# Sixteen graphs through a four-part layer on one core: the first and last six pipeline steps written out call by call, weight loads issued in another order

## Chip, cores and metric

One core of one Trainium2 chip. The metric is the device time of one execution in microseconds; the time before is the median of three runs.

## What is computed

The input is x, sixteen graphs of 512 nodes with 128 features, and adj, a 512 by 512 matrix of weights for each graph. Four parts follow each other, each a layer norm and ReLU, an operation on the graph, and a residual sum:

```
h = relu(norm(x));  x = x + attention(h, adj > 0.5)
    # 4 heads: e = leaky_relu(dst_i + src_j, 0.2), softmax over edges,
    # out = attn @ (h @ W) + bias
h = relu(norm(x));  x = x + max over 7 relations r of A_r @ (h @ W_r + c_r) + b
    # A_r: adj, its transpose, shifts, identity
h = relu(norm(x));  x = x + relu(D @ (adj + I) @ D @ (h @ W.T + b2))
h = relu(norm(x));  x = x + softplus(xn @ W_self + (I - S adj S') @ xn @ W_neigh)
    # xn = norm(h) * gamma + beta
```

## The kernel before

**Tiles.** A graph is a tile of 128 partitions by four blocks of 128 nodes. Its adjacency is 1 MB and comes in by one load into `adj_in` (two buffers), its features by another into `x_in` (two buffers). TensorE transposes the adjacency (`adjacency(t)`, L1200) and ScalarE copies it to `adj_tr` (three buffers, L551).

**Stages of a graph.** (1) Norm and hidden features (`norm0`, `rstd_0`, `hidden0`, `h0_transposed`), projection (`project`, L1221), the scores (`scores`, L892), the top score over all nodes (`top_rows`, `top_score`, `top_all`, L1240), the weights and values (`weights`, `values`), which are split into three bf16 parts (`part_hi`, `part_rest` L926, `part_mid` L621, `part_lo` L934). For each of the four heads a mask says which scores of an edge are positive: heads 0 and 2 on VectorE (L951, called masks here), heads 1 and 3 as signs on ScalarE (`sides`, L633) and one comparison on VectorE (L946). TensorE multiplies the parts with the non-edges (`no_edges`, L1290) and with each head's mask (`head(h)`, L1304), 48 matmuls each. `pair`, `attention`, `residual0`, `norm1` close the stage. (2) `hidden1`, the products A times h (`product_ah`, L1341) and A transposed times h (`product_ath`, L1350), the seven relations (`relation(k)`, L1372 to L1376), and the largest on VectorE (L1015). (3) `hidden2`, `h2_transposed` (L1386), `conv_bias`, `conv_linear` (L1403), `conv_in` (L537, the scaling to y2), `conv_product` (L1419), `conv_relu`. (4) `norm3`, `normal3`, `z_transposed`, `laplace_linear`, `laplace_product` (L1452), `softplus`, `result` (L488), `store`.

**Order.** Each engine has one stream, and semaphores join them. The kernel is a software pipeline written by hand: one loop over steps s for each engine, in which each call is made for graph s minus its stage's offset. So the order within a step is the same in all steps, and at the ends, calls for graphs that don't exist fall away:

```python
for s in range(GRAPHS + DEPTH - 1):       # TensorE, L1456, shortened
    product_ath(at(s - 3))
    ...
    head(3)(at(s - 2))
    laplace_product(at(s - 4))
    h2_transposed(at(s - 3))
```

Ahead of the loops stands the set-up. ScalarE issues the loads of the small weights: `w0c`, two broadcasts of the score vectors to 128 partitions, the edge weights, `w2_in`, the node mask, a broadcast of the first bias, and those of the last part. SyncE issues the graphs' loads and the large weights. TensorE transposes w2 and the mask and sums the edge rows (L1167 to L1171) once ScalarE's seventh load, the mask, has landed. VectorE makes the score columns (`head_weights`), then graph 0's statistics, then the edge rows in three bf16 parts (`edge_rows`, to L1109), two bias operations and a weight sum (`biases`, `laplace_weights`), all ahead of its loop.

## Time and profile before

| what | value |
|---|---|
| median of three runs | 727.64 us (727.63 to 728.45) |
| the profiled execution | 728.84 us |
| its span, first to last instruction | 726.7 us |
| TensorE busy in the span | 670.6 us, 92% |
| VectorE / ScalarE / GpSimd busy | 578.6 / 459.8 / 342.8 us |
| mean granted TensorE clock | 0.974 |
| mean rate of the transfers | 38 GB/s |

The profiled execution lasted 2.1 us longer than its span and 1.2 us longer than the median. A line of the order of time gives the start in us from the span's start, the busy time, the engine, the line of the kernel, what is written and read, and in brackets how long the engine was idle before and what ended that. Overlapping matmuls of a run are merged. The granted clock is a share of 2.4 GHz.

### The profile page before, as it was taken

How to read it: one execution, taken by the hardware profiler on the slowest of the kernel's cores; microseconds unless marked ns; L12 is line 12 of the kernel's file. 1: busy time of each engine (PE TensorE's matmuls, PEld its weight loads, DVE VectorE, ACT ScalarE, POOL GpSimd, SP SyncE). 2: the span in 40 equal slices, each digit the busy share in tenths (PEclk: the TensorE clock that was granted, in tenths of full speed). 3: DMA queues.
4: the chain of work that ended last, by engine and by line, in shares of the span. 5: the costliest groups of instructions: out<-in, count | busy, mean ns of one | idle time of the engine just before them, and what ended most of it. 6: DMA issues, size and time to landing. Idle time of an engine off the chain costs nothing. (4 is left out here: it accounts for less than half of the span.)

```text
span 726.7 us, 20537 instructions
## 1 busy us (share of the span) xinstructions
PE 670.6 (92%) x7714; PEld 550.7 (76%) x7730; DVE 578.6 (80%) x1726; ACT 459.8 (63%) x1137; POOL 342.8 (47%) x423
## 2 busy tenths in 40 slices
PE   2588899999999999999999999999999999999844
PEld 1585778889696978789796969788796969787533
DVE  2866988888889988888989988888989888886431
ACT  1455567767667577767667576767666676754332
POOL 1217255545546365555546265555556365353410
PEclk9779999999999999999999999999999999999987
DMA  8001101030202011020202011020302010000000
GB/s 232 1 3 41 35 23 53 0 88 3 88 3 87 3 39 52 1 89 2 88 3 87 3 48 43 0 91 1 89 2 88 3 62 14 16 2 16 1 15 14
DMA packets 28820, 27.83 MB, mean 38 GB/s; under 512 B 1517, under 2 KB 20530, under 8 KB 28722
## 3 DMA queue, kind: packets, MB, share of 16 engines
q1 hardware_dynamic: 27090, 25.97, 11.7%
q8 instruction: 62, 1.02, 0.6%
q10 hardware_dynamic: 1632, 0.55, 0.4%
q14 instruction: 36, 0.29, 0.1%
HBM read 22.31 MB, written 4.19 MB: 36 GB/s over the span
## 5 line engine op out<-in xcount | busy, mean ns | idle before, releaser
L387 POOL TENSOR_TENSOR rstd<-ve,half_neg 128x4 f32<-128x4 f32 x48 | 52.8, 1101 | 203.0 <-DVE ve L1034 116.3
L1304 PEld LDWEIGHTS ps<-part,pos 128*128 128x128 bf16 x3072 | 100.0, 98 | 3.2 <-DVE pos L946 0.7
L1304 PE MATMUL ps<-part,pos 128*128 128x66 bf16 x3072 | 101.8, 194 | 0.5 <-DVE pos L946 0.5
L951 DVE SCALAR_TENSOR_TENSOR pos<-ps,neg_s,none 128x512 bf16<-128x512 f32 x128 | 87.2, 744 | 10.7 <-issue 10.7
L1015 DVE TENSOR_REDUCE best<-ps 128x128 f32<-128x896 f32 x64 | 68.6, 1086 | 20.4 <-PE ps L1376 18.9
L633 ACT ACTIVATE side<-ps,sd 128x512 bf16<-128x512 f32 x128 | 77.2, 691 | 2.8 <-DVE pos L946 2.8
L1452 PE MATMUL ps<-u,adj_tr 128*128 128x128 f32 x512 | 61.1, 278 | 2.5 <-ACT u L731 2.5
L1452 PEld LDWEIGHTS ps<-u,adj_tr 128*128 128x128 f32 x512 | 58.4, 192 | 3.5 <-ACT u L731 3.5
L1290 PE MATMUL ps<-part,nmask 128*128 128x66 bf16 x1536 | 54.7, 197 | 6.0 <-DVE part L934 6.0
L1290 PEld LDWEIGHTS ps<-part,nmask 128*128 128x128 bf16 x1536 | 52.6, 99 | 9.9 <-issue 9.8
L1341 PE MATMUL ps<-adj_tr,h 128*128 128x512 f32 x128 | 59.4, 607 | 0.0
L1350 PE MATMUL ps<-adj_in,h 128*128 128x512 f32 x128 | 57.6, 592 | 0.0
L542 ACT ACTIVATE h<-x,off,rstd 128x128 f32<-128x128 f32 x128 | 53.2, 506 | 5.9 <-POOL off L390 5.9
L1375 PE MATMUL ps<-w_sb,h1t 128*128 128x384 f32 x128 | 51.7, 486 | 0.8
L1419 PE MATMUL ps<-y,adj_tr 128*128 128x128 f32 x384 | 52.2, 280 | 0.0
L418 POOL TENSOR_TENSOR rstd<-ve,half_neg 128x4 f32<-128x4 f32 x16 | 17.6, 1099 | 73.0 <-DVE ve L1057 73.0
L1419 PEld LDWEIGHTS ps<-y,adj_tr 128*128 128x128 f32 x384 | 48.2, 197 | 0.0
L946 DVE TENSOR_TENSOR pos<-side,none 128x2048 bf16<-128x2048 bf16 x32 | 39.2, 1226 | 9.3 <-PE ps L1304 9.0
L488 POOL TENSOR_TENSOR y_out<-sp,x 128x512 f32<-128x512 f32 x16 | 20.3, 1270 | 55.0 <-DVE sp L1078 55.0
L816 DVE BATCH_NORM_STATS2 st<-x 128x6 f32<-128x128 f32 x192 | 41.6, 279 | 0.7
L551 ACT ACTIVATE adj_tr<-ps 128x512 f32<-128x512 f32 x64 | 38.0, 608 | 4.7 <-PE ps L1200 4.7
L1341 PEld LDWEIGHTS ps<-adj_tr,h 128*128 128x128 f32 x128 | 23.2, 191 | 23.3 <-issue 23.0
(163 smaller groups left out, 1631.4 us busy)
## 6 DMA issues: line engine op xcount, KB each, us to landing
adj_in<-in_adj SPq DMA_DIRECT2D x16, 1024.0 KB, 6.2
x_in<-in_x SPq DMA_DIRECT2D x16, 256.0 KB, 6.5
out_y<-y_out SPq DMA_DIRECT2D x16, 256.0 KB, 6.7
w_sb<-in_L_gnn_W SPq DMA_DIRECT2D x7, 64.0 KB, 4.7
b_sb<-in_L_gnn_b SPq DMA_DIRECT2D x1, 256.0 KB, 8.7
c_rows<-c_parts SPq DMA_DIRECT2D x7, 1.5 KB
w0c<-in_L_gnn_W ACTq DMA_DIRECT2D x1, 64.0 KB, 3.0
a_bc<-in_L_gnn_a_src ACTq DMA_DIRECT2D x1, 64.0 KB, 6.4
```

The lines of the kernel that those rows point to most:

```text
L387: G.tensor_tensor(rstd[:], ve[:], half_neg[:, 0:T], ALU.pow).then_inc(power, 1)
L542: last = A.activation(dst[:, t, :], src[:, t, :], func, scale=scale[:, t:t + 1], bias=offset[:, t:t + 1])
L633: last = A.activation(side[:, t, :], bank(B_SPREAD[h]), ACT.Sign, bias=sd[:, t, 0, h:h + 1])
L951: last = V.scalar_tensor_tensor(pos[0][:, t, :], bank(B_SPREAD[h]), neg_s[:, t, h:h + 1], none[:, t, :], ALU.is_gt, ALU.is_gt)
L1015: V.tensor_reduce(best[:, k, :], ps[:, B_REL[k]:B_REL[k] + 2, :].rearrange("p a n -> p (a n)")[:, 0:RELS * F] .rearrange("p (r f) -> p f r ...
L1290: mm(ps[:, B_HEADS[q] + i // 2, o:o + 2 * VAL].rearrange("p (h v) -> p h v", h=2)[:, :, GRP:VAL], nmask[:, t, i * P:(i + 1) * P], parts[n] ...
L1304: last = mm(ps[:, B_HEADS[q] + i // 2, o:o + VAL], pos[h % 2][:, t, i * P:(i + 1) * P], parts[n][:, t, h, :], start=False, stop=(i % 2 == ...
L1341: last = mm(bank(B_AH), h1[:, t, :], adj_tr[g.three][:, t, :], start=(t == 0), stop=(t == T - 1))
L1350: last = mm(bank(B_ATH), h1[:, t, :], adj_in[g.two][:, t, :], start=(t == 0), stop=(t == T - 1))
L1375: mm(b, h1t[:, blk], w1_sb[:, 4:7, :], start=True, stop=False, skip_group_check=True)
L1419: last = mm(own, left, y2[:, t, :], start=(t == 0), stop=(t == T - 1))
L1452: last = mm(bank(B_AU)[:, i * F:(i + 1) * F], adj_tr[g.three][:, t, i * P:(i + 1) * P], u3[:, t, :], start=(t == 0), stop=(t == T - 1))
```

## The change

The loops now cover ten steps in the middle, with their calls in the same order. The first and the last six steps of each engine are written out as a list of calls, in orders of their own. The offsets grow by one (`DEPTH` 7, `at(s - 3)` becomes `at(s - 4)`), which changes no order by itself. Beside this:

- SyncE issues the last part's weights (four loads that ScalarE issued) behind the second adjacency. In its loop the load of an adjacency now stands behind the store; before, it stood ahead of features and store. The third x tile is loaded behind the edge rows.
- The two score vectors, the first bias and b2 are no longer broadcast by four loads of 64 KB. ScalarE loads them as four rows of 512 bytes ahead of its other loads, and one matmul with a row of ones spreads them over the partitions into PSUM (`broadcast_rows`).
- The sums of `b1` and of `w3` move from VectorE's set-up to GpSimd; the cast of the identity and the split of b2 move behind graph 0's scores on VectorE.
- `h1`, `h1t`, `aht`, `atht`, `sum_rows`, `y2` and `u3` get a second buffer; the four tiles of the softplus become slices of one tile, whose first partition holds the edge rows of the set-up.
- TensorE's waits are written anew for the changed orders; some are added that repeat others in the steady loop.

```diff
-DEPTH = 6
+DEPTH = 7
...
-        h1 = sb("h1", [P, T, F])
+        h1 = [sb(f"h1_{i}", [P, T, F]) for i in range(2)]
...
             load_features(at(0))
             load_adjacency(at(0))
-            load_features(at(1))
...
-            for s in range(2, GRAPHS + DEPTH - 1):
-                load_adjacency(at(s))
-                load_features(at(s + 1))
-                store(at(s - 4))
+            load_weights()
+            load_edge_rows()
+            for s in range(GRAPHS + 5):
+                load_features(later(s))
+                store(at(s - 5))
+                load_adjacency(later(s - 1))
...
+            for n, row in enumerate((a_src.rearrange("h f -> (h f)"), a_dst.rearrange("h f -> (h f)"), bias0, b2)):
+                act.dma_start(rows_in[0:1, n * F:(n + 1) * F], row.rearrange("(o f) -> o f", o=1)).then_inc(s_rows_in, 16)
             act.dma_start(w0c[:, 0:F], w0.rearrange("d h f -> d (h f)")).then_inc(s_heads, 16)
-            act.dma_start(a_bc[:, 0, :], a_src.rearrange("h f -> (h f)").partition_broadcast(P)).then_inc(s_heads, 16)
-            act.dma_start(a_bc[:, 1, :], a_dst.rearrange("h f -> (h f)").partition_broadcast(P)).then_inc(s_heads, 16)
...
+            def broadcast_rows():
+                pe.wait_ge(s_rows_in, 16 * 4)
+                pe.wait_ge(s_setup, 1)
+                mm(bank(B_ROWS_IN), ones_row[:], rows_in[:], start=True, stop=True).then_inc(s_rows_ps, 1)
```

**ScalarE, the start of graph 0 and of graph 1.** `h` is hidden features, `h0t` their transposes, `adj_tr` the transposed adjacency (x4: its four blocks), `side` the signs of a head, `part` a split part, `junk` the row sums of the adjacency. Before:

```order
L542 ACTIVATE h<-x_in,off,rstd 128x128 x4
L580 ACTIVATE h0t,h_sum<-ps 128x512
L551 ACTIVATE adj_tr,sums<-ps 128x512 x4
L589 COPY hv<-ps 128x512
L591 COPY mean<-ps 128x128
L598 ACTIVATE val<-s_rel,shift_c 128x16
L599 ACTIVATE val<-s_rel,shift_c 128x16
L633 ACTIVATE side<-ps,sd 128x512 x4
L614 CAST part<-val 128x1056
L621 CAST part<-rest 128x1056
L563 ACTIVATE junk,sums<-adj_in 128x512 x4
L542 ACTIVATE h<-x_in,off,rstd 128x128 x4
```

And now:

```order
L629 ACTIVATE h<-x_in,off,rstd 128x128 x4
L667 ACTIVATE h0t,h_sum<-ps 128x512
L638 ACTIVATE adj_tr,sums<-ps 128x512
L676 COPY hv<-ps 128x512
L678 COPY mean<-ps 128x128
L685 ACTIVATE val<-s_rel,shift_c 128x16
L686 ACTIVATE val<-s_rel,shift_c 128x16
L638 ACTIVATE adj_tr,sums<-ps 128x512 x3
L701 CAST part<-val 128x1056
L708 CAST part<-rest 128x1056
L720 ACTIVATE side<-ps,sd 128x512 x4
L650 ACTIVATE junk,sums<-adj_in 128x512 x4
```

The weights (`val`) come before three of the adjacency copies, and the signs of head 1 (the first `side`) stand behind both parts instead of ahead of them.

**VectorE, the last set-up before the loop, and graph 0's scores.** `w_both` is the weight sum of the last part, which followed the b2 split; `st`, `mv` and `ve` the statistics of graph 1, `sd` the scores, `none` and `nmask` the non-edges, `smax_t` the top score. Before:

```order
L1121 TENSOR_TENSOR w_both<-w_self,w_both 128x128
L816 BN_STATS st<-x_in 128x6 x4
L820 BN_AGGR mv<-st 128x2 x4
L830 TENSOR_SCALAR ve<-mv 128x4
L892 COPY sd<-ps 128x32
L895 TENSOR_REDUCE smax_p<-sd 128x4
L897 TENSOR_SCALAR neg_s<-sd 128x16
L838 TENSOR_SCALAR none<-adj_tr 128x2048
L904 TENSOR_REDUCE smax_t<-ps 4x1
```

And now, from the end of the edge rows (`c_parts`) to the weights:

```order
L1372 TENSOR_TENSOR c_parts<-late,c_parts 1x896
L1149 COPY sd<-ps 128x32
L1152 TENSOR_REDUCE smax_p<-sd 128x4
L1154 TENSOR_SCALAR neg_s<-sd 128x16
L1073 BN_STATS st<-x_in 128x6 x4
L1077 BN_AGGR mv<-st 128x2 x4
L1087 TENSOR_SCALAR ve<-mv 128x4
L1161 TENSOR_REDUCE smax_t<-ps 4x1
L1172 TENSOR_TENSOR s_rel<-sd,ps 128x16
```

The scores directly follow the edge rows; the statistics of graph 1 stand between them and the top score, and the non-edges come behind the weights.

**TensorE, the drain.** `h` with `ident` are the transposes of graph 14, `b_rows` and `w_t` its bias and linear part, `u` with `adj_tr` graph 13's last product, `y` the convolution of graph 14. Before:

```order
L1304 MATMUL ps<-part,pos 128x66 x144
L1452 MATMUL ps<-u,adj_tr 128x128 x16
L1386 MATMUL ps<-ident,h 128x128 x4
L1396 MATMUL ps<-b_rows,ones_b 128x512
L1403 MATMUL ps<-w_t,h2t 128x128 x4
L1419 MATMUL ps<-y,adj_own 128x128
L1419 MATMUL ps<-y,adj_tr 128x128 x4
```

And now:

```order
L1748 MATMUL ps<-part,pos 128x66 x96
L1856 MATMUL ps<-ident,h 128x128 x4
L1868 MATMUL ps<-b_rows,ones_b 128x512
L1877 MATMUL ps<-w_t,h2t 128x128 x4
L1934 MATMUL ps<-u_1,adj_tr 128x128 x16
L1895 MATMUL ps<-y_0,adj_own 128x128
L1895 MATMUL ps<-y_0,adj_tr 128x128 x4
```

Graph 13's last product moved from ahead of graph 14's transposes to behind its linear part.

## Rows read from the trace of the kernel before

**Rows 1.** Page, engines and slices: busy us (share) xinstructions; then tenths in 40 slices

```profile
PE 670.6 (92%) x7714; PEld 550.7 (76%) x7730; DVE 578.6 (80%) x1726; ACT 459.8 (63%) x1137; POOL 342.8 (47%) x423
...
PE   2588899999999999999999999999999999999844
...
PEclk9779999999999999999999999999999999999987
```

**Rows 2.** Stretches: length, busy us (xinstructions) of each engine, granted clock, DMA share, GB/s

```profile
0.00:13.40 13.40, 0.00 (x0) 0.00 (x0) 3.69 (x19) 1.28 (x1) 2.00 (x9) 1.00 0.80 214
...
39.00:44.30 5.30, 5.30 (x96) 5.30 (x97) 1.03 (x1) 5.00 (x13) 0.00 (x0) 0.50 0.01 5
...
98.40:139.10 40.70, 40.65 (x482) 33.60 (x482) 34.31 (x105) 27.82 (x69) 22.10 (x28) 1.00 0.10 34
...
654.50:667.10 12.60, 10.91 (x83) 10.33 (x80) 7.49 (x33) 6.17 (x15) 4.19 (x7) 0.86 0.00 1
```

**Rows 3.** Order of time (start, us, what, idle before): set-up, scores, top score

```profile
13.48 0.45 PE L1167 MATMUL ps<-ident,w_in 128*128 128x128 f32 x1 [13.48 <-DMA mask_in<-in_nodemask]
...
22.23 1.08 DVE L1109 TENSOR_TENSOR c_parts<-c_left,c_parts 1x896 bf16<-1x896 f32 x1
...
27.30 0.18 DVE L892 COPY sd<-ps 128x32 f32<-128x32 f32 x1
...
30.48 0.59 PE L1240 MATMUL ps<-ident,smax_t 4*128 4x4 f32 x2
```

**Rows 4.** Order of time, 31.80 to 41.87: signs of head 1, parts, first product

```profile
31.80 2.40 ACT L633 ACTIVATE side<-ps,sd 128x512 bf16<-128x512 f32 x4
...
35.23 1.26 DVE L926 TENSOR_TENSOR rest<-val,part 128x1056 f32<-128x1056 f32 x1 [1.01 <-ACT part L614]
...
37.63 1.26 DVE L934 TENSOR_TENSOR part<-rest,part 128x1056 bf16<-128x1056 f32 x1 [1.14 <-ACT part L621]
...
38.99 2.88 PE L1290 MATMUL ps<-part,nmask 128*128 128x66 bf16 x48 [6.03 <-DVE part L934]
```

**Rows 5.** Order of time, 49.31 to 64.96: head 3, statistics, attention, A times h

```profile
49.31 1.61 PE L1304 MATMUL ps<-part,pos 128*128 128x66 bf16 x48
...
52.31 0.86 DVE L816 BATCH_NORM_STATS2 st<-x_in 128x6 f32<-128x128 f32 x4
...
53.71 0.24 DVE L985 RECIPROCAL rden<-den 128x16 f32<-128x16 f32 x1
...
61.00 3.96 PE L1341 MATMUL ps<-adj_tr,h 128*128 128x512 f32 x8
```

**Rows 6.** Order of time, graph 1's heads: TensorE's two gaps

```profile
85.67 1.62 PE L1304 MATMUL ps<-part,pos 128*128 128x66 bf16 x48 [0.48 <-DVE pos L946]
...
88.72 0.66 PE L1386 MATMUL ps<-ident,h 128*128 128x128 f32 x4 [1.43 <-ACT h L542]
```

**Rows 7.** Order of time, a steady graph: GpSimd, VectorE's low part, TensorE

```profile
274.24 1.27 POOL L481 TENSOR_TENSOR x1b<-x,b_sb 128x512 f32<-128x512 f32 x1
...
274.59 2.04 DVE L934 TENSOR_TENSOR part<-rest,part 128x1056 bf16<-128x1056 f32 x1
...
277.05 1.66 PE L1290 MATMUL ps<-part,nmask 128*128 128x66 bf16 x48
```

**Rows 8.** Order of time, the drain, 658.15 to 676.31: TensorE, and ScalarE's hidden features

```profile
658.15 0.60 PE L1386 MATMUL ps<-ident,h 128*128 128x128 f32 x4
...
661.82 0.49 PE L1419 MATMUL ps<-y,adj_own 128*128 128x128 f32 x2 [1.23 <-ACT y L537]
...
662.84 1.65 ACT L542 ACTIVATE h<-x,off,rstd 128x128 f32<-128x128 f32 x4 [1.07 <-POOL off L390]
...
665.78 0.39 PE L1419 MATMUL ps<-y,adj_own 128*128 128x128 f32 x2
...
666.90 0.39 PE L1419 MATMUL ps<-y,adj_own 128*128 128x128 f32 x2
...
675.64 0.67 PE L1372 MATMUL ps<-w_sb,aht 128*128 128x256 f32 x2 [0.77 <-ACT atht L671]
```

More of the change, by code:

```diff
@@ L187, in graph_kernel @@
         h2t = sb("h2t", [P, N])
[L188 removed]
+        y2 = [sb(f"y2_{i}", [P, T, F]) for i in range(2)]
         r2 = sb("r2", [P, T, F])
@@ L654, in h1_transposed @@
                 act.wait_ge(h1t_ps, g.all(1))
-                if g.has(1):
-                    act.wait_ge(hw_ps, g.before(1).all(T))
-                A.copy(h1t[:], bank(B_H1T)).then_inc(h1t_sb, 1)
+                if g.has(2):
+                    act.wait_ge(hw_ps, g.before(2).all(T))
+                A.copy(h1t[g.two][:], bank(B_H1T)).then_inc(h1t_sb, 1)
             @of_graph
@@ L661, in product_ah @@
                 act.wait_ge(ah_ps, g.all(1))
-                if g.has(1):
-                    act.wait_ge(hw_ps, g.before(1).all(T))
-                A.copy(aht[:], bank(B_AH)).then_inc(aht_sb, 1)
+                if g.has(2):
+                    act.wait_ge(hw_ps, g.before(2).all(T))
+                A.copy(aht[g.two][:], bank(B_AH)).then_inc(aht_sb, 1)
             @of_graph
@@ L668, in product_ath @@
                 act.wait_ge(ath_ps, g.all(1))
-                if g.has(1):
-                    act.wait_ge(hw_ps, g.before(1).all(T))
-                A.copy(atht[:], bank(B_ATH)).then_inc(atht_sb, 1)
+                if g.has(2):
+                    act.wait_ge(hw_ps, g.before(2).all(T))
+                A.copy(atht[g.two][:], bank(B_ATH)).then_inc(atht_sb, 1)
             @of_graph
@@ new lines, in _ @@
+            attention(at(0))
+            scores(at(1))
+            residual0(at(0))
+            norm1(at(0))
+            unit_columns()
+            top_score(at(1))
+            weights(at(1))
+            no_edges(at(1))
+            node_scales(at(0))
+            head(0)(at(1))
+            degrees(at(1))
+            norm0(at(2))
+            head(1)(at(1))
+            part_rest(at(1))
+            edges_negative(at(1))
+            largest(0)(at(0))
+            largest(1)(at(0))
+            part_lo(at(1))
@@ new lines, in _ @@
+            largest(2)(at(0))
+            largest(3)(at(0))
+            residual1(at(0))
+            norm2(at(0))
+            head(2)(at(1))
+            pair(0)(at(1))
+            head(3)(at(1))
+            norm0(at(3))
+            pair(1)(at(1))
+            attention(at(1))
+            residual0(at(1))
+            norm1(at(1))
+            scores(at(2))
+            no_edges(at(2))
+            top_score(at(2))
+            weights(at(2))
+            head(0)(at(2))
+            residual2(at(0))
@@ new lines, in _ @@
+            residual1(at(12))
+            head(2)(at(13))
+            norm2(at(12))
+            node_scales(at(12))
+            head(3)(at(13))
+            pair(0)(at(13))
+            pair(1)(at(13))
+            attention(at(13))
+            residual0(at(13))
+            degrees(at(13))
+            laplace(at(11))
+            norm1(at(13))
+            scores(at(14))
+            top_score(at(14))
+            softplus(at(11))
+            weights(at(14))
+            no_edges(at(14))
@@ new lines, in _ @@
+            attention(at(14))
+            laplace(at(12))
+            node_scales(at(13))
+            residual0(at(14))
+            norm1(at(14))
+            scores(at(15))
+            degrees(at(14))
+            softplus(at(12))
+            top_score(at(15))
+            weights(at(15))
+            no_edges(at(15))
+            residual2(at(13))
+            head(0)(at(15))
+            edges_negative(at(15))
+            part_rest(at(15))
+            norm3(at(13))
+            largest(0)(at(14))
@@ new lines, in _ @@
+            h1_transposed(at(0))
+            product_ath(at(0))
+            spread(2)(at(1))
+            spread(3)(at(1))
+            relation(0)(at(0))
+            relation(1)(at(0))
+            relation(2)(at(0))
+            relation(3)(at(0))
+            no_edges(0)(at(1))
+            head(0)(at(1))
+            head(1)(at(1))
+            no_edges(1)(at(1))
+            head(2)(at(1))
+            adjacency(0)(at(2))
+            h2_transposed(at(0))
+            head(3)(at(1))
+            conv_bias(at(0))
```

1113 lines of the change are left out of this document (850 added, 263 removed).

## The prediction

> **What bounds the kernel now.** I read the page first, then the table of stretches, then the order of time at both ends. The page says TensorE is busy 670.6 us of the span of 726.7; its busy digits are low only in the first three slices and the last four, and so are those of its granted clock [rows 1]. The table of stretches makes this exact: from one graph to the next, 98.40 to 139.10, TensorE is busy 40.65 of 40.70 us [rows 2]. Sixteen such periods are 651 us. The change writes the steady loop down unchanged except for SyncE and some waits, so what can be won lies in the other 76 us: the fill (to about 98 us) and the drain (from about 654 us). In the fill TensorE does nothing for 13.4 us, and from 39.0 to 44.3 it works at half clock (granted 0.50, so 1.2 of 2.4 GHz) [rows 2]. A gain needs TensorE to arrive earlier at a point from which it runs without gaps; I follow graph 0 to that point.
>
> **Part 1, until the first product over the non-edges.** TensorE's set-up starts at 13.48, when the node mask lands [rows 3]. Its load was seventh in ScalarE's queue and is now ninth, behind four short rows in place of two broadcasts. Issues there take about half a microsecond (the bound: nothing, if the queue is held up elsewhere, or 2 us); I take 1.0 later. The set-up to the last split of the edge rows takes 13.48 to 23.31 (22.23 + 1.08) [rows 3]; plus one more copy, 0.2, it ends at 24.5. Before, eleven more VectorE operations and the statistics of graph 1 stood ahead of the scores, which began at 27.30 [rows 3]. Now the scores come at once, at 24.5: 2.8 earlier. The statistics (1.4 us, as from 52.31 to 53.71 in rows 5) now stand between scores and top score, so the top score's matmul comes at 24.5 + 0.5 + 1.4 + 0.4 = 26.8, where it was at 30.48 [rows 3]: 3.7 earlier. From there the old chain went values, high part, rest, middle part, low part, to 38.89 (37.63 + 1.26), and TensorE started at 38.99 after 6.03 idle [rows 4]. With 3.7 less this would be 35.3. But one step is moved against it: the signs of head 1 (2.40 us on ScalarE [rows 4]) ran at 31.80, beside GpSimd's values; now they stand behind the middle part, and the first product waits for them. The middle part ends about when the low part begins, so the signs end 2.4 - 1.3 = 1.1 after the low part. Net: 3.7 - 1.1 = 2.6.
>
> A price stands against this. Where GpSimd ran a two-input operation from 274.24, VectorE's low part took 2.04 us [rows 7] in place of 1.26 [rows 4]. In graph 0 of the old kernel GpSimd was idle there; now its bias for graph 1 and its diagonal blocks of graph 0 are moved there. Bounds: nothing, or 0.8 for each of rest and low part, 1.6; I take 0.6, since the diagonal blocks are four short pieces. Part 1 gives **2.0** (bounds 0 and 4). "GPSIMD Engine Reference" of the Trainium skill (its table of properties) says that GpSimd's SBUF interfaces are shared with VectorE and contend when VectorE has two SBUF inputs; rest and low part are such. By that rule taken whole, every meeting costs, and Part 1 would give 1.0; the row agrees that a meeting can cost 0.8.
>
> **Part 2, from there to graph 0's first relation product.** The transposes of graph 1's hidden features go from before head 3 to behind it: about 0.4 (four matmuls in 0.60 [rows 8], less what they overlap). Head 3 began at 49.31 and ended at 50.92 [rows 5]. VectorE then did the statistics of graph 2 from 52.31 ahead of attention, at 53.71 [rows 5]; they are gone from there, 1.4, and the scores of graph 1 are put in ahead of the residual, 0.5: +0.9. ScalarE now sums graph 1's rows ahead of graph 0's hidden features, four activations of the size of the signs' four (2.40 [rows 4]). I count no cost: they are covered by VectorE's attention and statistics and GpSimd's offset, which graph 0's hidden features wait for anyway, and by my count both strands end together. If that cover fails, it costs up to 1 us. TensorE started that product, A times h, only at 61.00 [rows 5], 0.7 after the hidden features were there, because of four spreads it does earlier now: +0.7 of which I count 0.5. Part 2: 0.4 + 0.9 + 0.5 = **1.8** (bounds 0 and 2.5).
>
> **Part 3, graph 1's heads.** The gaps of 0.48 and 1.43 us [rows 6] are waits for head 3's mask and for graph 0's second hidden features. Head 2's mask was before the second statistics and is now behind them, so the features come earlier by the length of that mask, and the adjacency transpose is moved between: both gaps go, 1.9. Late next is graph 2's low part: VectorE there has 13 us of work in the 16 us from A times h to the first product, and steady state already meets it with little room (low part done at 276.63, TensorE at 277.05 [rows 7]). I count **1.2** (bounds 0 and 1.9).
>
> The doubled buffers (h1, its transposes and products, y2, u3) take away waits that the steady table shows nobody is held by: nothing. SyncE's adjacency load is now behind the store; in the steady loop the store's result is ready before TensorE's product, for which the load waits in both orders, so the load starts when it did: nothing. "Issued at once": no big load was held by anything before either, only the third x tile by its buffer: nothing. The result buffers' overlay and the moved bias sums: nothing, on GpSimd while it waits.
>
> **Part 4, the drain.** In the old order TensorE did graph 13's last product before graph 14's transposes (658.15) and then waited for the linear part and its scaling, to 661.82 [rows 8]. In the stretch 654.5 to 667.1 the granted clock was 0.86 [rows 2]. The four blocks of the convolution began at 661.82 and 665.78 (the third) and the fourth's last piece at 666.90 [rows 8]: the first two took 3.96 together, the third 1.12, so the low clock cost 3.96 - 2.24 = 1.7. Now the transposes and the linear part stand ahead of graph 13's last product, whose 3.65 us (654.50 to 658.15) hide the scaling (1.23 idle goes). The wait for the transposed copy, 0.45, stays. Gain 1.2 + 1.7 = 2.9. Graph 15's first hidden features were ready at 664.49 (662.84 + 1.65 [rows 8]) and come about 1 us earlier now, since its statistics no longer stand behind graph 13's final sum; TensorE arrives at 664.2. From the last block's end to the first relation product it was 666.90 to 675.64 [rows 8], 8.7 us, the two products swapped and again one copy waited for (0.77). Behind it everything is one chain in the same order, and keeps its length. Part 4: **2.9** (bounds 1.2, if the clock falls anyway, and 3.3). "TensorE: Matmul & The Clock Gate" of the Trainium skill (Part 1) says that an idle TensorE falls to half rate and a busy one returns to full. By that rule the remaining 0.45 us might leave the clock up, as I count; the trace agrees in that 0.86 follows the two waits.
>
> **Sum.** 2.0 + 1.8 + 1.2 + 2.9 = 7.9. The profiled execution took 728.84, so 720.9 for one like it; the median of the runs is 727.64, 1.2 below it, so I forecast **719.7**.
>
> **The rivals.** (A) *Only the drain and half the fill.* What ScalarE does in the hand-written steps stands in the way where I took it as covered: Part 2 and Part 3 give nothing, Part 1 gives 1.0. Then 727.6 - 3.9 = 723.7. For it: by my count ScalarE's strand around 50 us has no room to spare, and two signs calls have moved. Chance 0.2. (B) *Better than that*: the masks land no later, no ports meet, every gap goes: 4.0 + 2.5 + 1.9 + 3.3 = 11.7, 716.0. Chance 0.12. (C) *Slower: the steady period grows.* VectorE's low part is ready 0.4 us before TensorE wants it [rows 7]; the store now issues some 5 us earlier and the fill hands the loop another phase between GpSimd and VectorE. If the low part comes over 0.4 us later in every graph, TensorE waits in each: 1.3 later gives 0.9 in 11 graphs, 9.9 in all, against the gain of 7.9: 729.6. It decides from 1.1 us on. Against it: TensorE is the clock of this loop, and its order is unchanged. Chance 0.04. (D) *The change does not do what it says*: the loads were never held, and an order by hand that only repeats the pipeline leaves the ends as they are: 727.6. Against it: I found each gap moved. Chance 0.03.
>
> **How the numbers follow.** My forecast has 0.61, A 0.2, B 0.12, C 0.04, D 0.03. A measurement of this kernel can tell about 0.2% (1.5 us) from no change. Faster by more: 0.61 + 0.2 + 0.12 = 0.93; the same 0.03 (D); slower 0.04 (C). The range takes in A and most of B: 716.3 to 724.0.
>
> **What would show it.** Right: period 40.7 again; scores of graph 0 near 24.5; first product over non-edges near 37; A times h of graph 0 near 57; no gap of over 0.3 us in graph 1's heads; the convolution of graph 14 in 3.6 us at full clock; the distance from its last piece to the end unchanged at some 59.8 us. Wrong: a first product after 38.5 (Part 1), a gap before A times h (Part 2), a clock under 0.95 in the drain's convolution (Part 4), or any period over 40.8 (C).

## The result, and the profile after

| | before | after |
|---|---|---|
| median of the runs | 728.05 us (727.63 to 729.01, 4 runs) | 724.17 us (723.51 to 725.77, 4 runs) |
| ratio, 95% interval | | 0.9947 (0.9929 to 0.9964) |
| the profiled execution / its span | 728.84 / 726.7 us | 725.77 / 724.0 us |
| TensorE busy in the span | 670.6 us | 674.4 us |

The change makes the kernel 3.9 us faster, about half of the 7.9 I forecast. On the page, TensorE is busy longer in a shorter span. Against [rows 1], its clock digits are lower at the end (76 for 87), and at the start one of them is higher (799 for 779):

```profile
PE 674.4 (93%) x7732; PEld 550.6 (76%) x7732; DVE 582.0 (80%) x1727; ACT 458.7 (63%) x1137; POOL 345.8 (48%) x425
...
PE   4579999999999999999999999999999999999834
...
PEclk9799999999999999999999999999999999999976
```

The order of time of the changed kernel, in its fill, answers to [rows 3 to 6]. The rows are the first transpose of the set-up, the scores, the top score's matmul, the signs of head 1, the low part, the first product over the non-edges, A times h of graph 0, two products of graph 1's heads, and the first relation product of graph 1:

```profile
10.91 0.48 PE L1606 MATMUL ps<-ident,w_in 128*128 128x128 f32 x1 [2.41 <-DMA mask_in<-in_nodemask]
...
20.90 0.17 DVE L1149 COPY sd<-ps 128x32 f32<-128x32 f32 x1
...
24.32 0.38 PE L1681 MATMUL ps<-ident,smax_t 4*128 4x4 f32 x2
...
31.90 2.41 ACT L720 ACTIVATE side<-ps,sd 128x512 bf16<-128x512 f32 x4
32.02 1.70 DVE L1191 TENSOR_TENSOR part<-rest,part 128x1056 bf16<-128x1056 f32 x1 [0.53 <-ACT part L708]
...
34.45 1.75 PE L1734 MATMUL ps<-part,nmask 128*128 128x66 bf16 x28 [5.65 <-ACT side L720]
...
54.71 5.40 PE L1788 MATMUL ps<-adj_tr,h 128*128 128x512 f32 x8 [2.25 <-ACT h L629]
...
78.71 1.61 PE L1748 MATMUL ps<-part,pos 128*128 128x66 bf16 x48 [0.26 <-DVE pos L1208]
...
81.64 1.62 PE L1748 MATMUL ps<-part,pos 128*128 128x66 bf16 x48 [0.41 <-DVE pos L1203]
...
101.23 0.67 PE L1840 MATMUL ps<-w_sb,aht 128*128 128x256 f32 x2 [0.45 <-ACT atht L760]
```

Everything is early: the set-up by 2.6 us, the scores by 6.4, the product over the non-edges by 4.5, A times h by 6.3. But A times h takes 5.40 us where it took 3.96 [rows 5], after a wait of 2.25 that was not there. The stretches of the two, the changed kernel's and that of before, have a granted clock of 0.68 and of 0.93 (columns as in [rows 2]):

```profile
54.70:60.10 5.40, 5.39 (x10) 2.33 (x11) 4.84 (x7) 2.66 (x6) 5.05 (x5) 0.68 0.00 0
```

```profile
61.00:64.96 3.96, 3.96 (x11) 1.95 (x11) 3.41 (x8) 3.29 (x7) 3.88 (x6) 0.93 0.00 0
```

The later rows of the same view show a steady graph (A times h and its first relation product), a new gap ahead of graph 13's fourth group of relations, and the last piece of graph 14's convolution:

```profile
255.85 3.70 PE L1788 MATMUL ps<-adj_tr,h 128*128 128x512 f32 x8
...
264.40 0.67 PE L1840 MATMUL ps<-w_sb,aht 128*128 128x256 f32 x2
...
581.42 0.28 DVE L1161 TENSOR_REDUCE smax_t<-ps 4x1 f32<-4x128 f32 x1 [3.63 <-PE ps L1676]
...
597.96 0.70 PE L1840 MATMUL ps<-w_sb,aht 128*128 128x256 f32 x2 [0.94 <-DVE best L1272]
...
660.96 0.39 PE L1895 MATMUL ps<-y,adj_own 128*128 128x128 f32 x2
```

Stretches of the changed kernel: a steady graph, the written step of graph 13's relations and graph 14's heads, the convolutions of graphs 14 and 15, and the last product (columns as in [rows 2]):

```profile
133.43:174.23 40.80, 40.70 (x483) 33.60 (x482) 36.35 (x106) 28.35 (x72) 25.43 (x30) 1.00 0.16 47
...
582.72:624.74 42.02, 40.97 (x484) 33.60 (x483) 35.00 (x101) 30.96 (x80) 22.23 (x25) 1.00 0.13 39
...
657.60:661.20 3.60, 3.60 (x35) 3.60 (x34) 2.11 (x11) 2.21 (x6) 1.24 (x3) 1.00 0.00 0
689.30:694.80 5.50, 5.47 (x32) 5.28 (x32) 0.69 (x1) 1.73 (x3) 1.27 (x1) 0.69 0.13 39
710.80:716.10 5.30, 5.23 (x32) 5.04 (x32) 0.03 (x1) 0.43 (x1) 0.00 (x0) 0.72 0.00 0
```

A steady graph takes 40.80 where it took 40.70 [rows 2], that written step 42.02, and two products of the end run at 0.69 and 0.72 of the full clock. The same event in both traces, subtracted, gives the balance of the profiled executions:

| up to | before | after | ahead by | change |
|---|---|---|---|---|
| A times h, graph 1 | 98.41 | 92.34 | 6.07 | +6.07 |
| A times h, graph 11 | 505.36 | 500.79 | 4.57 | -1.50 |
| A times h, graph 13 | 586.75 | 582.72 | 4.03 | -0.54 |
| A times h, graph 14 | 627.45 | 624.74 | 2.71 | -1.32 |
| last piece of graph 14's convolution | 666.90 | 660.96 | 5.94 | +3.23 |
| end of the span | 726.7 | 724.0 | 2.7 | -3.24 |

In these two executions, then, the ends won 9.3 us, and 6.6 were lost at three places that my sum did not have: the steady period, the written step around 597 us, and the clock at the very end. The experiments take these apart.

### The profile page after: what moved, and what is told of

Read it like the earlier page. It is cut to its first block and busy times, and to the rows that moved or that the text cites. A ratio compares the mean times of both kernels' runs of the same rounds, so it can differ in the third digit from the quotient of the medians.

```text
span 724.0 us, 20626 instructions
## 1 busy us (share of the span) xinstructions
PE 674.4 (93%) x7732; PEld 550.6 (76%) x7732; DVE 582.0 (80%) x1727; ACT 458.7 (63%) x1137; POOL 345.8 (48%) x425
## 5 line engine op out<-in xcount | busy, mean ns | idle before, releaser
L1934 PEld LDWEIGHTS ps<-u,adj_tr 128*128 128x128 f32 x512 | 59.8, 196 | 3.6 <-ACT u L820 3.6
L500 POOL TENSOR_TENSOR y_out<-late,x 128x512 f32<-128x512 f32 x16 | 20.3, 1268 | 54.1 <-DVE late L1335 54.1
L461 POOL TENSOR_TENSOR val<-hv,val 128x512 f32<-128x512 f32 x32 | 35.8, 1138 | 17.2 <-ACT val L686 17.2
L1840 PE MATMUL ps<-w_sb,aht 128*128 128x256 f32 x128 | 39.5, 390 | 3.9 <-DVE best L1272 0.9
```

The costliest lines, as they stand in the source:

```text
L1934: last = mm(bank(B_AU)[:, i * F:(i + 1) * F], adj_tr[g.three][:, t, i * P:(i + 1) * P], u3[g.two][:, t, :], start=(t == 0), stop=(t == T - 1))
```

## The experiments

**The changed kernel again (r1_after).** No edit.

> The changed kernel again, unchanged. It ran 724.17 us against 728.05 (ratio 0.9947). Every theory expects the same period of 40.81 us from one graph's product A times h to the next, the same gap of 0.94 us ahead of relation(3) of graph 13, and about 724 us; if the low clock of the last part (conv_product and laplace_product of graph 15, 3 us longer than before the change) is chance, at least one of the two comes back to 3.6 to 3.8 us here; if it belongs to the change, both stay above 5 us.

Measured: 723.82 us (723.53 to 725.14, 6 runs), ratio to before 0.9939 (0.9925 to 0.9954). Period 40.81, 42.03 for the written step, the gap of 0.95 again. The stretches of the two products at the end are now at full clock:

```profile
690.30:694.20 3.90, 3.84 (x32) 3.65 (x32) 0.69 (x1) 1.78 (x4) 1.25 (x1) 1.00 0.02 4
...
709.90:713.90 4.00, 3.84 (x32) 3.65 (x32) 0.07 (x1) 0.48 (x2) 0.00 (x0) 1.00 0.00 0
```

The 3 us at the end do not belong to the change. This execution paid elsewhere: from A times h of graph 0 to graph 1's took 38.34 us, against 37.63 in the first profile, so A times h of graph 1 starts at 93.25, only 5.16 ahead of the kernel before. The losses in the middle are the same to 0.1 us (532.40 and 532.52 us from A times h of graph 1 to graph 14's), so they are real; at the end of the span this execution is 5.0 us ahead.

Two profiles of one kernel thus differ in the fill, and this limits what a single one can tell. There are seven profiles with this fill (the first, this one, e1, e2, e3, e6, e7; in e1, e6 and e7 one repeated wait is out): the first product over the non-edges starts between 33.43 and 34.56 us, A times h of graph 1 between 90.96 and 93.40. From A times h of graph 1 to graph 15's convolution the agreement is far better (596.96 and 597.11 us in the two profiles of the changed kernel). Times of the next kernels are set against this run's 723.82. They were run in four groups; in these the kernel before had medians of 728.48 (r1 to e3), 728.21 (e4 to e7), 728.33 (e8 to e10) and 728.19 us (e11), so across groups 0.3 us means nothing.

**One wait fewer (e1_one_wait).**

```diff
                         else:
-                            pe.wait_ge(h1t_sb, g.all(1))
                             pe.wait_ge(side_ok, g.after(1).th(1, 2))
```

> One wait is taken out of relation(0) for all graphs but the last: the second wait for h1t, which waits on a semaphore that TensorE has already waited for in product_ah, so nothing is left unguarded. Theory W (the period grew from 40.69 to 40.81 because a further wait stands in TensorE's queue behind the wait for the A transposed times h copy): period back to 40.69 to 40.72, 11 graphs by 0.1 = 1.1 to 1.3 us faster than the changed kernel, about 722.9. Rival L (the low part or a port costs it): period stays 40.81 and the time stays at 724.

Measured: 721.34 us (720.28 to 724.27), ratio 0.9909 (0.9890 to 0.9928). The period is that of before. In the order of time, A times h and the first relation product of a graph:

```profile
255.18 3.70 PE L1788 MATMUL ps<-adj_tr,h 128*128 128x512 f32 x8
...
263.62 0.67 PE L1839 MATMUL ps<-w_sb,aht 128*128 128x256 f32 x2
```

and the stretch from this A times h to the next:

```profile
255.18:295.87 40.69, 40.64 (x483) 33.59 (x483) 35.95 (x106) 28.47 (x72) 21.62 (x26) 1.00 0.12 41
```

The distance between the two rows is 8.44 us, against 8.55 with the wait (264.40 - 255.85) and 8.45 before the change (269.64 - 261.19). The weight load of the relation product starts 0.32 us after the end of ScalarE's copy of A transposed times h with the wait, and 0.21 without. Theory W holds, and L falls: nothing else was altered. From A times h of graph 1 to that of graph 14 it is 531.03 us instead of 532.40, so 1.4 us; the median is 2.5 us lower, of which the trace explains that 1.4.

**The old order for graph 14's heads (e2_late_step_loop).** The loops run two steps longer on all engines; only the last step group, from graph 15's heads on, stays written out.

```diff
-            for s in range(6, GRAPHS + DEPTH - 1 - 6):
+            for s in range(6, GRAPHS + DEPTH - 1 - 4):
```

> Graph 14's heads are taken from the old loop order again; only the last step from graph 15's heads on is written out. Theory O (the written order puts top score ahead of the non-edges of graph 14 and delays the largest of graph 13, which makes TensorE wait 0.94 us and makes that graph 42.02 us in place of 40.81): that graph takes 40.8 us, the drain's gain stays, 1.2 us faster than the changed kernel, 723.0. Rival (the drain's gain of 3.2 us comes out of this order): the 1.2 us come back as a gap at graph 14's convolution, and the time stays at 724.

Measured: 726.71 us (725.05 to 728.84), ratio 0.9977 (0.9966 to 0.9988): 2.9 slower than the repeat, against both theories. TensorE's waits in the order of time:

```profile
624.56 0.38 PE L1545 MATMUL ps<-ident,smax_t 4*128 4x4 f32 x2 [0.95 <-DVE smax_t L1082]
...
641.19 0.70 PE L1704 MATMUL ps<-w_sb,aht 128*128 128x256 f32 x2 [2.02 <-DVE best L1193]
```

The gap ahead of the relations was not removed but put off by one graph, and doubled: it goes with the seam between loop and written list, or with the written step itself. That step takes 41.83 us and the next 42.46, where the changed kernel has 42.03 and 40.12. From A times h of graph 1 to graph 15's convolution it is 598.87 us, against 596.96 and 597.11: the trace explains 1.8 to 1.9 of the 2.9.

**Start written out, end as a loop (e3_fill_only).**

```diff
-            for s in range(6, GRAPHS + DEPTH - 1 - 6):
+            for s in range(6, GRAPHS + DEPTH - 1):
```

> The written-out start stays, the loops run to the end as before the change. Theory (fill and drain are separate terms: fill +6.1, steady -2.0 with the old loop for the last graphs, drain +3.2 and the written step of graph 14 -1.3): gives back 3.2 and wins 1.3, so 1.9 slower than the changed kernel, about 726.1, and conv_product of graph 14 shows the low clock again. Rival (the end of the program costs the gain by its low clock whatever the order): conv_product and laplace_product of graph 15 stay above 5 us; else, if the written drain caused that, they return to 3.6 and 3.8 and the time is 723 to 724.

Measured: 724.22 us (722.57 to 725.43), ratio 0.9938 (0.9922 to 0.9954): the same as the repeat with its 723.82. The whole written drain brings nothing that can be told in the time; from A times h of graph 1 to graph 15's convolution it brings 0.3 to 0.5 us (597.45 here). The stretches of the step that had 42.02 us, and of graph 14's convolution:

```profile
582.75:623.55 40.80, 40.64 (x483) 33.60 (x483) 34.20 (x97) 28.48 (x73) 18.97 (x23) 1.00 0.11 34
658.00:661.90 3.90, 3.88 (x36) 3.87 (x37) 0.48 (x3) 2.80 (x7) 0.92 (x3) 1.00 0.00 0
```

and in the order of time the start of that convolution:

```profile
658.02 0.49 PE L1665 MATMUL ps<-y,adj_own 128*128 128x128 f32 x2 [1.23 <-ACT y L584]
```

TensorE waits the same 1.23 us as before the change [rows 8], and the clock behind it is 1.00. The stretch of the old kernel had 0.69:

```profile
661.80:667.30 5.50, 5.48 (x36) 5.47 (x37) 1.18 (x4) 3.43 (x7) 1.09 (x4) 0.69 0.00 0
```

So the clock there did not need the wait hidden. The low products of graph 15 went both ways: convolution 5.5 us, last product 3.84.

**Four broadcasts back (e4_broadcasts_back).** Four loads of 64 KB into a tile that nothing reads, two on ScalarE ahead of `edge_t`, one there behind the mask, one on SyncE behind `b1`:

```diff
+            act.dma_start(spare_bc[:, 0, :], a_src.rearrange("h f -> (h f)").partition_broadcast(P)).then_inc(s_spare, 16)
+            act.dma_start(spare_bc[:, 1, :], a_dst.rearrange("h f -> (h f)").partition_broadcast(P)).then_inc(s_spare, 16)
```

> The changed kernel with the four 64 KB broadcast loads added again at their old places in the queues of ScalarE and SyncE, into a tile that nothing reads; the rows and the matmul that spreads them stay. It measures what the removed broadcasts cost. Theory B (they held up the queues: in the profile of before the issue of w_edge took 2.39 us on ScalarE and that of a later broadcast 2.38 us on SyncE, and the mask landed at 13.48): TensorE's transposes of the set-up start at 13 or later instead of 10.9, scores of graph 0 near 23.5 instead of 20.9 to 21.3, about 2 us slower than the changed kernel, 726. Rival P (the prediction's: broadcasts cost their half microsecond of issue and nothing else): scores 1.0 us later at most, 724.5 to 725.

Measured: 726.72 us (724.92 to 728.19), ratio 0.9977 (0.9964 to 0.9989): 2.9 slower than the repeat. The order of time shows the mask's load held for 2.26 us at its issue, and the set-up waiting for it until 13.90:

```profile
5.81 2.26 ACTq L626 DMA_DIRECT2D mask_in<-in_nodemask  x1
...
13.90 0.48 PE L1613 MATMUL ps<-ident,w_in 128*128 128x128 f32 x1 [5.51 <-DMA mask_in<-in_nodemask]
```

Scores at 23.89, A times h of graph 1 at 95.06. Theory B holds: the set-up starts 2.6 to 3.0 us later than in the two profiles of the changed kernel, and A times h of graph 1 2.7 (1.8) later, so the four short rows in place of the broadcasts bring some 2 to 3 us of the fill's gain.

**New loads, old order at the start (e5_loop_start).** The loops begin at step 1 again; the written end stays, and VectorE's bias rows stand ahead of the loop.

```diff
-            hidden0(at(0))
-            h0_transposed(at(0))
...
-            for s in range(6, GRAPHS + DEPTH - 1 - 6):
+            for s in range(1, GRAPHS + DEPTH - 1 - 6):
```

> New loads and new set-up, but from graph 1's statistics on the old loop in place of the written-out start; the written end stays. It splits the fill's gain of 6.1 us into loads and orders. Theory: earlier loads give 2.6 and the set-up without eleven VectorE operations up to 2; the orders (top score, statistics behind attention, head masks) the rest, 1.5 to 2.5. So product A times h of graph 0 comes at 56.5 to 57.5 instead of 54.8, that of graph 1 about 94 to 95 instead of 92.1 to 93.2, time near 726. Rival (the loads do it all): same times as the changed kernel at graph 1, 724.

Measured: 728.56 us (726.39 to 730.71), ratio 1.0002 (0.9988 to 1.0017): nothing is left of the gain. TensorE in the order of time, at graph 0's non-edges and in graph 1's heads:

```profile
37.13 2.88 PE L1553 MATMUL ps<-part,nmask 128*128 128x66 bf16 x48 [6.03 <-DVE part L1081]
...
84.08 1.62 PE L1567 MATMUL ps<-part,pos 128*128 128x66 bf16 x48 [0.47 <-DVE pos L1093]
...
87.17 0.66 PE L1675 MATMUL ps<-ident,h 128*128 128x128 f32 x4 [1.47 <-ACT h L598]
```

Both gaps of [rows 6] are back, to 0.04 us, and the wait of 6.03 of [rows 4]. A times h of graph 1 comes at 96.86: 1.6 earlier than before the change, 4.5 (3.6) later than in the two profiles of the changed kernel, and later than in any of the seven. So the orders of the start carry more than my expectation gave them, and with the steady waits and the written step left in, loads alone would not have paid.

**Loops to the end, one move of the drain kept (e6_tail_of_loop).** From e1 and e3:

```diff
-                laplace_product(at(s - 5))
+                if s != 18:
+                    laplace_product(at(s - 5))
...
                 mean_value(at(s - 2))
+                if s == 18:
+                    laplace_product(at(s - 5))
                 conv_product(at(s - 4))
```

On VectorE `laplace` moves behind `norm1` in the same step.

> Written-out start as changed, the repeated wait taken out, loops to the end on all engines; of the written drain only one move is kept: graph 13's last product stands behind graph 14's linear part on TensorE, and its sum behind the statistics of graph 15 on VectorE. Theory O (the written drain wins by this one move and loses 1.3 us in graph 13 by the early top score): no gap ahead of relation(3) of graph 13, all periods 40.70 to 40.80 up to graph 13, graph 14's convolution with no wait of 1.23, about 1.2 us faster than the kernel with the one wait removed (721.3), 720.1. Rival (the drain's gain comes from the whole written order): the 1.2 us come back between graph 14's convolution and graph 15's relations, 721.3 or more.

Measured: 722.27 us (720.63 to 722.82, 5 runs), ratio 0.9919 (0.9901 to 0.9937). The time can't be told from e1's 721.34. The stretch of the former written step, and TensorE's waits ahead of graph 14's transposes and linear part:

```profile
579.66:620.35 40.69, 40.69 (x483) 33.59 (x482) 34.32 (x97) 28.48 (x73) 18.98 (x23) 1.00 0.11 34
```

```profile
648.01 0.66 PE L1628 MATMUL ps<-ident,h 128*128 128x128 f32 x4 [0.43 <-ACT h L589]
...
649.34 1.16 PE L1649 MATMUL ps<-w_t,h2t 128*128 128x128 f32 x8 [0.39 <-ACT h2t L735]
```

The 1.3 us are back, the wait of 1.23 is gone and 0.43 is new. From A times h of graph 1 to the start of graph 15's convolution it takes 594.71 us (685.67 - 90.96), against 595.50 with e1 (687.59 - 92.09): 0.8 of the expected 1.2. It is the balance of both moves: what the loop order saves in graph 13, less what it costs in graph 14. The profile's last product took 5.32 us at the lower clock, which hides it in the time.

**TensorE kept busy at the end (e7_waits_and_busy).** e1, with matmuls that nothing reads:

```diff
+            def keep_busy(n, first=False):
+                if first:
+                    pe.wait_ge(best_ok, at(15).all(T))
+                for _ in range(n):
+                    mm(bank(0), ones_b[:], c_rows[:, 0:512], start=True, stop=True)
...
+            keep_busy(34)
             z_transposed(at(15))
```

> The kernel with the one repeated wait removed, plus matmuls in TensorE's waits of the last two parts whose results are not read (55 of 128x512, bf16), which keep TensorE busy ahead of laplace_product(14), conv_linear(15), conv_product(15), z_transposed(15), laplace_linear(15) and laplace_product(15). Theory K (TensorE's clock falls in these waits, and the matmuls behind them pay: transposes of z 1.11 in place of 0.60, linear part 3.7 in place of 1.99, and by chance conv_product 5.4 for 3.8 and the last product 5.2 for 3.8): granted clock 1.00 behind the waits, 2.3 us faster than with the waits empty at the least, 719.0 or less, and a smaller spread of the runs. Rival: they run at half clock as well and push the work behind them back, 722 or more.

Measured: 720.17 us (719.76 to 720.20, 4 runs), ratio 0.9886 (0.9869 to 0.9904). From the convolution's end to the last product's start it is 13.79 us instead of 16.04 (e1). Of z's transposes the order of time shows

```profile
701.83 0.66 PE L1905 MATMUL ps<-ident,z 128*128 128x128 f32 x4 [1.71 <-ACT z L629]
```

where every run without the filling has 1.11 or 1.12 us, and the linear part behind it takes 1.99 instead of 3.8. The runs spread over 0.4 us, those of e1 over 4.0. What theory K says of the clock holds, though the median gains 1.2 and not 2.3, and 720.17 misses its 719.0; this profile lost 0.8 us in the fill (38.31 us from A times h of graph 0 to graph 1's, 37.51 in e1). That the clock is what makes the runs differ fits the spread, but it is not shown: there are four runs only, and those of the changed kernel in r1 spread by 1.6 without any filling.

**Signs between the parts (e8_signs_first).**

```diff
             part_hi(at(0))
-            part_mid(at(0))
             sides(1)(at(0))
+            part_mid(at(0))
```

> The changed kernel with the signs of head 1 of graph 0 put between the high and the middle part on ScalarE, where ScalarE waits 2.03 us for VectorE's rest; now they stand behind the middle part, and TensorE's first product over the non-edges waits for them to 33.5 to 34.5 (both write PSUM bank 2). Theory S (the place of the signs costs the 0.6 us between the end of the low part at 32.95 and the product at 33.69): the middle part comes 0.4 us later, the product follows the low part, net 0.2 to 0.4 us earlier, 723.5 to 723.8, the same within what can be told. Rival (they cost the 1.1 us of my forecast): product at 32.6, 1.1 us faster, 722.7.

Measured: 724.33 us (723.11 to 725.67), ratio 0.9948 (0.9934 to 0.9963): the time shows nothing. In the order of time the first product follows the low part:

```profile
32.95 2.87 PE L1734 MATMUL ps<-part,nmask 128*128 128x66 bf16 x48 [5.50 <-DVE part L1191]
```

In the repeat the signs were what it waited for:

```profile
33.69 2.54 PE L1734 MATMUL ps<-part,nmask 128*128 128x66 bf16 x42 [4.84 <-ACT side L720]
```

Counted from the top score's matmul, it takes 9.50 us to this product (32.95 - 23.45) instead of 10.14 in the repeat and 10.13 in the first profile: 0.6 us earlier, between the two expectations. A times h of graph 1 comes at 90.59, but that says little: e6, with the signs in their old place, had it at 90.96. At the end this profile lost 1.8 us in its last product (5.62 us) again.

**TensorE kept busy at the start (e9_busy_start).** e1, with 4, 9 and 4 matmuls of 128x512 in f32 in the three waits of graph 0.

```diff
+            def keep_busy_0(n):
+                for _ in range(n):
+                    mm(bank(0), ident[:], adj_in[0][:, 0, :], start=True, stop=True)
```

> The kernel with the one repeated wait removed (721.3 us), plus 17 matmuls of 128x512 (f32, 0.46 us each at full clock, result not read) in TensorE's three waits of the fill: 4 ahead of the last spreads of graph 0, 9 ahead of the first product over the non-edges, 4 ahead of A times h of graph 0. Theory K (in the fill the clock is at half after each long wait: the product over the non-edges took 2.9 in place of 1.66 us, the first masks' products 2.83 for 1.62, A times h 5.4 for 3.65): granted clock 1.00 from 33 us on, A times h of graph 0 at 53 and 3.7 us long, graph 1's at 90 in place of 92.1 to 93.2, 2 to 3 us faster, 719, and a smaller spread. Rival Q (the filling matmuls run at half clock themselves, 0.9 us each, and come behind the wait's end): first product over the non-edges at 38, 3 us slower, 724.

Measured: 722.29 us (721.02 to 722.73, 4 runs), ratio 0.9919 (0.9905 to 0.9933), not faster than e1. The order of time tells why:

```profile
29.24 7.03 PE L1939 MATMUL ps<-adj_in,ident 128*128 128x512 f32 x16
35.68 1.45 PE L1939 MATMUL ps<-adj_in,ident 128*128 128x512 f32 x3
36.97 1.66 PE L1734 MATMUL ps<-part,nmask 128*128 128x66 bf16 x48
```

The clock is up, as theory K has it (the product takes 1.66 us), but one such matmul takes 0.86 us, not 0.46: the rows count an f32 matmul twice, so the x8 of A times h are four matmuls. Nine of them overrun the wait and push the product to 36.97. Against e1 that product is 2.45 us later and A times h of graph 1 (92.44) only 0.35, so the full clock won 2.1 us and the overrun ate it. From the product to A times h of graph 1 it is 55.47 us here, and 57.33 to 59.67 in the seven profiles without filling.

**All parts (e10_all_parts).** e6, with e7's and e9's filling.

> All that helped in one kernel: the repeated wait out, loops to the end with graph 13's last product behind graph 14's linear part, matmuls whose result is not read in the waits of the last two parts and in the three of the fill. If the terms add: from 721.3 us (one wait out) 0.8 for the old order of graph 13, 1.2 to 2.2 for the clock at the end, 2 to 3 for the clock in the fill: 715 to 717. If the fill's filling costs (rival Q of the run before), 719 to 722.

Measured: 718.30 us (717.63 to 718.79, 4 runs), ratio 0.9864 (0.9849 to 0.9879): between the two cases, as the overrun of e9 is in it (first product over the non-edges at 37.39). All periods from graph 2 to graph 13 are 40.69 to 40.71.

**All parts, sized (e11_all_parts_sized).** e10 with 2, 6 and 2 matmuls in the fill, and the signs as in e8.

```diff
-            keep_busy_0(9)
+            keep_busy_0(6)
```

> As the kernel with all parts (718.3 us), but with the fill's matmuls sized by what the last runs showed of one (0.86 to 0.90 us, not 0.46, for 128x512 in f32): 2, 6 and 2 in the three waits in place of 4, 9 and 4, and with the signs of head 1 between the high and the middle part, so that the first product over the non-edges waits for the low part alone. Theory K: that product at 33.0 to 33.3 in place of 37.4, full clock from there, A times h of graph 0 at 52 to 53 in 3.6 us, graph 1's at 88 to 89 in place of 92.9, 4 to 5 us faster, 713.5 to 714.5. Rival (the clock falls all the same, since the filling leaves gaps of 0.4 us): as in the run with the signs alone, graph 1's at 90.6, 716.

Measured: 715.59 us (715.02 to 716.68, 5 runs), ratio to before **0.9832** (0.9818 to 0.9845). It beats both kernels, by 12.6 and by 8 to 9 us, but misses the upper end of its expectation by 1.1, and the time alone lies nearer to the rival's 716; the clock and the starts below are what speaks for theory K. Its clock digits, the order of time around A times h of graph 0, and the stretches of graph 0's heads and of the last product:

```profile
PEclk9999999999999999999999999999999999999998
```

```profile
32.99 1.66 PE L1507 MATMUL ps<-part,nmask 128*128 128x66 bf16 x48 [0.36 <-issue]
...
53.25 3.70 PE L1561 MATMUL ps<-adj_tr,h 128*128 128x512 f32 x8 [0.55 <-ACT h L589]
```

```profile
33.00:43.40 10.40, 9.12 (x287) 8.87 (x288) 9.71 (x23) 4.83 (x13) 2.44 (x6) 1.00 0.10 30
...
701.40:705.30 3.90, 3.84 (x32) 3.65 (x32) 0.00 (x0) 0.48 (x2) 0.00 (x0) 1.00 0.01 4
```

A times h of graph 1 starts at 89.07, 9.3 us before that of the old kernel, 1.9 before e6's and 1.5 before the 90.59 of the signs alone. Of the 5.6 us between the spans of e6's profile and this one, the other 3.7 lie behind the start of graph 15's convolution. How much the moved signs add to the filling was not tried alone.

## Why the prediction was right or wrong

The direction was right, the size twice too large. The step that failed is the one that put everything between fill and drain at nothing: it cost 3.4 us up to graph 14. The fill gave at least what I said, in part for other reasons, and the drain gave its sum only with luck in the clock.

**Part 1, forecast 2.0, measured 4.5 (5.3 in the repeat).** The step "mask ninth in the queue, 1.0 later" had the wrong sign: it landed 2.6 earlier (13.48 to 10.91). I counted issues and took each as half a microsecond; before the change, issues beside the broadcasts took 2.39 us on ScalarE and 2.38 on SyncE, and that of the mask itself 1.21:

```profile
2.87 2.39 ACTq L523 DMA_DIRECT2D w_edge<-in_L_gnn_W  x1
...
6.86 1.21 ACTq L525 DMA_DIRECT2D mask_in<-in_nodemask  x1
```

e4 shows that the broadcasts hold such issues up. The scores came at 20.90, 3.6 before my 24.5, and the mask was 3.6 before my 14.5. From the scores to the top score's matmul it then took 3.4 us where I had 2.3, and from that matmul to the first product 10.13 where I had 10.2: 3.6 less 1.1 is the 2.5 by which Part 1 was too small. The 1.1 is that execution's: in the repeat the same way took 2.2 us (21.33 to 23.55), and nearly the whole surplus is the mask's. The signs were the last to end, as I said, but 0.6 us after the low part, not 1.1. The price for GpSimd beside VectorE, 0.6, was about right for the parts (the low part took 1.70 instead of 1.26), and I missed it on the b2 split, one cast of which took 1.10 us beside GpSimd's values; before, with GpSimd idle, it took 0.22:

```profile
25.73 1.10 DVE L1054 CAST b_parts<-b_left 128x128 bf16<-128x128 f32 x1
```

The two-input operation behind it took 1.06 for 0.29. `part_rest` then began 0.7 us after the high part had ended (28.89 to 29.63), so that my 10.2 was met by errors that cancel. "GPSIMD Engine Reference" of the Trainium skill (its table of properties) has the contention for VectorE's operations with two inputs in SBUF and for those in a 2-port mode; the trace agrees for the two-input ones, and whether the cast ran in such a mode no row shows.

**Part 2, forecast 1.8, measured 1.75 (0.8 in the repeat).** From the first product to A times h it was 22.01 us and is 20.26. Yet I had named a gap ahead of A times h as a sign against this part, and there is one of 2.25: the hidden features are later than TensorE in any case, so the sum held while TensorE idles instead of doing the spreads later.

**Part 3, forecast 1.2, measured -0.2 (-0.9 in the repeat).** The mechanism was right: e5 brings back 0.47 and 1.47 us with the old order, and with the written order there are waits of 0.26 and 0.41 in the place of these 1.9, though I had allowed none of over 0.3. What failed is that I did not ask what the new wait of 2.25 does to the clock: A times h took 5.40 us for 3.96, and 37.63 - 1.44 = 36.19 would have been the 1.2 gained (37.41 before). With the waits filled it is 35.73 to 35.82 (e9 to e11).

**The steady loop, forecast 0, measured -1.5 up to graph 11.** The step that failed is "written down unchanged except for SyncE and some waits": I had seen that waits were added that repeat others, and gave them no price because none of them holds anyone. One costs 0.11 us in each graph (e1). Another 0.3 in graph 1 is a new wait of 0.45 for the copy of A transposed times h. I had bound rival C to VectorE's low part; the slower period came, but neither by its mechanism nor in its size. The other periods, 40.9 and 41.0 in the graphs of the written steps, fall to 40.70 when the loops run on and the repeated wait is out (e6, e10); which of the calls costs them stays open.

**The step I did not read, -1.3.** My sum of the drain began at 654 us, but the written order begins two graphs before. In graph 13's relations TensorE waits 0.94 us for VectorE's largest. e3 and e6 show that the written order causes it; that VectorE stands 3.63 us before graph 14's top score and is late from there is read from the trace and was not tried alone.

**Part 4, forecast 2.9, measured 3.2, in part by luck.** The convolution ran in 3.6 us at full clock, and the wait of 1.23 is gone. But of my two terms, the 1.7 for the clock was not the order's to win: e3 has the old waits and the full clock. "TensorE: Matmul & The Clock Gate" of the Trainium skill (Part 1) says that an idle TensorE falls to half rate. The trace agrees that it can: the wait of 1.23 us was followed by 0.69 before the change and by 1.00 in e3, and ahead of graph 15's convolution the same kernel had 0.69 behind it in its first profile and 1.00 in the repeat. So what such a wait costs differs from one execution to the next. What the order is worth at the full clock can be read from A times h of graph 13 to the last piece of graph 14's convolution: 80.15 us before the change, 78.73 in e3 with the old order and the full clock, 78.24 with the written order, and 77.60 in e6. So 1.4 of the gain came with the clock, the whole written order is worth 0.5, and e6's one move some 0.9, when 0.2 are taken off for the wait that it lacks in two graphs.

**Behind it, forecast unchanged.** From the last piece to the end I had 59.8 us. It was 63.0 in the first profile and 59.7 in the repeat (721.7 - 662.01). The chain is unchanged; 3.0 of the 3.2 are the lower clock in two products, 5.47 and 5.23 us for 3.84.

Rival A had the size almost right (723.7) and the reason wrong: up to A times h of graph 1 the fill gave 6.1 us, and 5.2 in the repeat, where I had forecast 5.0 and the rival 1.0. SyncE's order and the doubled buffers were not tried apart; the period that returns to 40.69 with one wait out leaves them no cost. Two slips changed nothing: VectorE's operations between the edge rows and graph 1's statistics, which I counted as eleven, are ten in the order of time, and rival B's terms give 715.9, not 716.0.

## What to carry to other kernels

Price what a change adds to a steady loop first, however small: 0.11 us in each round took 1.4 of the 9.3 us that the ends had won, and at the end of the program the old loop order served as well as the one written by hand. Where TensorE waits at the ends, count the work behind the wait at both levels of its clock. Where nothing useful can be put into the wait, matmuls that nothing reads are worth trying, sized by a measured one and no longer than the wait: with them and the moved signs 722.3 us (e6) became 715.6 (e11). And before one profile is set against another, see how far two of the same kernel differ at that place: here by up to 2.4 us at the end of the fill.

## What the runs showed of the hardware

- A wait on a semaphore that has long been reached cost TensorE's queue 0.11 us behind a wait that binds (8.55 against 8.44 us; the period of the steady graphs 40.81 against 40.70).
- Four broadcast loads of 64 KB held issues of unrelated loads in their queue for up to 2.4 us, and a mask of the set-up by 2.6 to 3.0 us; rows of 512 bytes were issued in 0.23 to 0.53 us each, and one matmul spread them in 2.04 us.
- The granted clock behind the same wait differs from one execution to the next: behind 1.23 us it was 0.69 or 1.00. The runs of the kernels here without filling spread by 1.6 to 4.3 us (4 to 12 runs each); with the end filled it was 0.4 (e7), 1.2 (e10) and 1.7 (e11), with 4 or 5 runs each, too few to show that filling narrows it.
- A cast of 128x128 on VectorE took 0.22 us with GpSimd idle and 1.10 us beside a two-input operation of GpSimd, in every profile with that order.
